# Softmax exponents moved ahead of a copy, a ranking round split by rows, and token factors in one piece, in the first stage of a fused attention kernel

## What is computed

```
Q = x @ Wq;  K = ctx @ Wk;  V = ctx @ Wv
scores = Q K^T / sqrt(32)                  # per head, 256 x 256
topv, topi = top_k(scores, 32)             # per row
probs = softmax(topv), scattered to topi   # the other 224 places are 0
c_t = mean over heads of probs, times V, times the text mask
x1 = layernorm(x) * (1 + gate*scale_in(c_t)) + gate*shift_in(c_t)
y  = s4d(x1)                               # a convolution over the whole sequence, by a DFT
xt = x + y * (1 + gate*scale_out(c_t)) + gate*shift_out(c_t)
out = layernorm(xt + gelu(layernorm(xt) @ W1 + b1) @ W2 + b2)
```

## Time and profile before

| | |
|---|---|
| median of 3 runs | 1389.21 us |
| the profiled execution, its own time | 1390.56 us |
| its span, first to last instruction | 1388.9 us |
| granted TensorE clock, mean over the span | 0.925 |
| busy: PE / DVE / ACT / POOL | 85% / 63% / 44% / 33% |
| first stage | from 0 to about 456 us of the span |
| start of turns 0, 1, 2, 3 (PE L1235) | 118.4, 152.8, 192.8, 231.5 us |
| start of turns 4, 5, 6, 7 | 271.5, 311.4, 350.1, 389.0 us |

### The profile page before, as it was taken

How to read it: one execution, slowest core, us unless ns; L and a number is a source line. 1 busy time by engine, 2 the same in 40 slices (tenths; PEclk the granted TensorE clock), 3 DMA queues, 4 the chain that set the end, 5 groups by cost and what they waited for, 6 DMA issues and landing times. The chain is left out here.

```text
span 1388.9 us, 24448 instructions
## 1 busy us (share of the span) xinstructions
PE 1181.3 (85%) x7032; PEld 854.2 (62%) x7032; DVE 876.4 (63%) x2513; ACT 611.6 (44%) x1242; POOL 451.4 (33%) x669
## 2 busy tenths in 40 slices
PE   1588799999896588789998949689999899999997
PEld 1385567777675477577766837456666555555554
DVE  7998888888842466656574647557676425353534
ACT  3545565666541223557763327256666521211120
POOL 2266144334446108837337337422220000000000
PEclk9858999999898899999999969779999999999999
DMA  9000000000000463486737516351010000000000
GB/s 280 9 2 1 1 1 1 1 1 1 1 1 1 111 221 100 136 269 217 261 112 254 171 45 106 92 146 16 9 17 1 1 1 1 15 0 15 0 16 16
DMA packets 92461, 91.98 MB, mean 66 GB/s; under 512 B 27056, under 2 KB 77746, under 8 KB 92340
## 3 DMA queue, kind: packets, MB, share of 16 engines
q1 hardware_dynamic: 80052, 65.32, 15.4%
q0 software_dynamic: 12288, 25.18, 7.1%
HBM read 75.79 MB, written 14.68 MB: 65 GB/s over the span
## 5 line engine op out<-in xcount | busy, mean ns | idle before, releaser
L3544 ACT ACTIVATE m_silu<-m_psG 128x512 f32<-128x512 f32 x48 | 28.7, 597 | 215.2 <-PE m_psU L3664 215.2
L3597 DVE TENSOR_TENSOR m_act<-m_silu,m_psU 128x512 f32<-128x512 f32 x48 | 33.0, 688 | 122.5 <-ACT m_silu L3544 107.7
L2304 PE MATMUL gq_psH<-gq_xT,gq_w 128*128 (+1 forms) x564 | 98.6, 300 | 5.2 <-issue 3.0
L2304 PEld LDWEIGHTS gq_psH<-gq_xT,gq_w 128*128 128x128 f32 x564 | 78.9, 200 | 31.0 <-issue 26.0
L2314 PE MATMUL gq_psY<-leaf_w,gq_hT 128*128 (+1 forms) x282 | 89.5, 400 | 7.2 <-DVE gq_hT L2190 6.8
L3664 PE MATMUL m_psG<-m_xnT,m_gate 128*128 128x512 f32 x192 | 92.0, 602 | 2.1 <-PEq L192 2.1
L3664 PE MATMUL m_psU<-m_xnT,m_up 128*128 128x512 f32 x192 | 90.6, 594 | 0.0
L2190 DVE SCALAR_TENSOR_TENSOR gq_hT<-gq_xT,unit_leaf,gq_act 128x128 f32<-128x128 f32 x141 | 49.6, 352 | 49.6 <-ACT gq_act L2022 33.0
L3075 DVE TENSOR_REDUCE c_max<-c_psA 128x4 f32<-128x1024 f32 x32 | 39.2, 1226 | 60.9 <-PE c_psA L3226 60.9
L1906 POOL DMA_INDIRECT gq_x<-rows_x,gq_token_i x48 | 46.2, 963 | 93.9 <-DVE gq_tile_row L2183 54.3
L205 POOL TENSOR_SCALAR m_rstd<-m_mean_var 128x4 f32<-128x4 f32 x4 | 0.9, 231 | 232.5 <-DVE m_mean_var L1389 232.5
(11 more groups left out here) (584 smaller groups left out, 3034.3 us busy)
## 6 DMA issues: line engine op xcount, KB each, us to landing
leaf_w<-in_group_w SPq DMA_DIRECT2D x128, 128.0 KB, 3.9
leaf_w<-in_group_w SPq DMA_DIRECT2D x64, 256.0 KB, 5.0
a_w<-in_L_xattn_W SPq DMA_DIRECT2D x2, 1024.0 KB, 11.9
rows_x<-token_rows SPq DMA_DIRECT2D x8, 256.0 KB, 5.2
sorted_y_q<-gq_y SPq DMA_DIRECT2D x16, 128.0 KB, 4.5
sorted_y_k<-rows_ahead SPq DMA_DIRECT2D x16, 128.0 KB, 5.4
sorted_y_v<-gq_y SPq DMA_DIRECT2D x16, 128.0 KB, 1.8
rows_f<-token_rows SPq DMA_DIRECT2D x8, 256.0 KB, 2.8
```

Source lines behind the costliest of these rows:

```text
L2304: last = pe.matmul(psH[n % 2][:, 0:P], w1[n % 3][:, c, :], xT[:, c, bass.ds(g * -P + u * P, P)], start=(c == 0), stop=(c == DC - 1))
```

## The change

On ScalarE `projected` is parted into `x_turned` (L656) and `projected` (L660), and the exponentials of the ranked scores now stand between the two, in two halves, each waiting for its own half of `ranked`. In round 3 on VectorE `ranked` is raised behind the fourth and the eighth MAX8; the shares are computed by halves: four takes, shares of half 0, two takes, shares of half 1, two takes. `scaled_shares` waits for each half of the shares by itself. On GpSimd the token factors of batches 0 to 6 are computed in one piece of 14 columns in turn 9; the piece at the end of turn 7 is gone. No other operation, shape or buffer changes, and no DMA. The convolution itself is not touched.

```diff
@@ -358,8 +358,8 @@
         v_ps, v_sb = sig("a_v_ps"), sig("a_v_sb")
         score_ps, score_sb = sig("a_score_ps"), sig("a_score_sb")
         first8, left, taken = sig("a_max"), sig("a_left"), sig("a_taken")
-        exps, ranked, etop_sb = sig("a_exps"), sig("a_ranked"), sig("a_etop")
-        shares, scaled, mean_sb = sig("a_shares"), sig("a_scaled", 2), sig("a_mean")
+        exps, ranked, etop_sb = sig("a_exps"), sig("a_ranked", 2), sig("a_etop", 2)
+        shares, scaled, mean_sb = sig("a_shares", 2), sig("a_scaled", 2), sig("a_mean")
         at_ps, at_sb = sig("a_attnT_ps"), sig("a_attnT_sb")
         ct_ps, ct_sb = sig("a_ctT_ps"), sig("a_ctT_sb")
         fin_ps, fout_ps, fout_sb = sig("a_film_in_ps"), sig("a_film_out_ps", ST), sig("a_film_out", ST)
@@ -500,7 +500,7 @@
                             do.mark(biased)
                         else:
                             biased.then_inc(last_biased, 1)
-                            next_factors(NEXT - 2, NEXT)
+                            next_factors(0, NEXT)
                         released(pool, o_sb, z)
                         root(1, o_var, o_rs, z)
                         if z == B - 1:
@@ -527,8 +527,6 @@
                         do(pool.tensor_tensor(yspec[:, 1, :], prod[:, 2, :], prod[:, 3, :],
                                               ALU.add))
                         pool.tensor_copy(yspec[:, 0, 0:1], yspec[:, 0, 0:1]).then_inc(y_sb.s, 1)
-                    if m == B - 1:
-                        next_factors(0, NEXT - 2)
 
                 pool.memset(core.ident[:], 0.0).then_inc(core.setup, 1)
                 pool.memset(core.ones_bf[:], 1.0).then_inc(core.setup, 1)
@@ -651,25 +649,28 @@
                                               bias=nmax[:, j:j + 1], scale=scale)
                     last.then_inc(exps.s, 1)
 
-                def projected(f):
+                def x_turned(f):
                     reached(act, xT_ps, f)
                     act.activation(xnT[:], pA[:], ACT.Copy).then_inc(xT_sb.s, 1)
+
+                def projected(f):
                     reached(act, proj_ps, f)
                     released(act, score_ps, f)
                     own = slice(0, 2 if f < 2 else 1)
                     act.activation(qk[:, own], pB[:, own], ACT.Copy).then_inc(proj_sb.s, 1)
 
                 def top_exponents(b):
-                    reached(act, ranked, b)
-                    for j in range(R):
-                        last = act.activation(etop[:, j, :], top[:, j, :], ACT.Exp,
-                                              bias=nmax[:, j:j + 1], scale=scale)
-                    last.then_inc(etop_sb.s, 1)
+                    for n in range(2):
+                        reached(act, ranked, b, n + 1)
+                        for j in range(n * HALF, (n + 1) * HALF):
+                            last = act.activation(etop[:, j, :], top[:, j, :], ACT.Exp,
+                                                  bias=nmax[:, j:j + 1], scale=scale)
+                        last.then_inc(etop_sb.s, 1)
 
                 def scaled_shares(b):
-                    reached(act, shares, b)
                     reached(act, exps, b)
                     for n in range(2):
+                        reached(act, shares, b, n + 1)
                         for j in range(n * HALF, (n + 1) * HALF):
                             last = act.activation(prob[:, j, :], prob[:, j, :], ACT.Copy,
                                                   scale=einv[:, j:j + 1])
@@ -738,9 +739,12 @@
                     if has(e):
                         gelus(e, range(HC // 2, HC))
                     if has(f):
+                        x_turned(f)
+                    if has(b):
+                        top_exponents(b)
+                    if has(f):
                         projected(f)
                     if has(b):
-                        top_exponents(b)
                         scaled_shares(b)
                     if has(f):
                         scores_out(f)
@@ -761,6 +765,7 @@
                 act.activation(tmask[:], tmask8[:], ACT.Copy, scale=1.0 / H0).then_inc(masks, 1)
                 x_normal(0)
                 values_out(0)
+                x_turned(0)
                 projected(0)
                 act.wait_ge(core.loads[0], 16)
                 sums(1)
@@ -769,6 +774,7 @@
                 film_folded()
                 x_normal(1)
                 values_out(1)
+                x_turned(1)
                 projected(1)
                 for n in range(B // 2 - 1):
                     keys_out(n)
@@ -819,7 +825,7 @@
                         do.wait_apart()
                     for j in range(R):
                         last = dve.max(top[:, j, 8 * r:8 * r + 8], row_in(r, j))
-                        if r == 3 and j == R - 1:
+                        if r == 3 and j % HALF == HALF - 1:
                             last.then_inc(ranked.s, 1)
                         else:
                             do.mark(last)
@@ -839,13 +845,14 @@
                     if signal is not None:
                         last.then_inc(signal.s, 1)
 
-                def shares_of(b):
-
-                    reached(dve, etop_sb, b)
-                    do(dve.tensor_reduce(einv[:], etop[:], AX_X, ALU.add))
-                    do(dve.reciprocal(einv[:], einv[:]))
-                    tm = tmask[:, b * ST:(b + 1) * ST].unsqueeze(1).to_broadcast([P, H0, ST])
-                    e3 = einv[:].rearrange("p (h t) -> p h t", h=H0)
+                def shares_of(b, n):
+
+                    q = slice(n * HALF, (n + 1) * HALF)
+                    reached(dve, etop_sb, b, n + 1)
+                    do(dve.tensor_reduce(einv[:, q], etop[:, q], AX_X, ALU.add))
+                    do(dve.reciprocal(einv[:, q], einv[:, q]))
+                    tm = tmask[:, b * ST:(b + 1) * ST].unsqueeze(1).to_broadcast([P, H0 // 2, ST])
+                    e3 = einv[:, q].rearrange("p (h t) -> p h t", t=ST)
                     dve.tensor_tensor(e3, e3, tm, ALU.mult).then_inc(shares.s, 1)
 
                 def pairs_of(b):
@@ -913,8 +920,10 @@
                         eight(b, 3)
                         reached(dve, ranked, b)
                         take(3, range(HALF))
-                        shares_of(b)
-                        take(3, range(HALF, R), taken)
+                        shares_of(b, 0)
+                        take(3, range(HALF, R - 2))
+                        shares_of(b, 1)
+                        take(3, range(R - 2, R), taken)
                         pairs_of(b)
 
                 def next_stats(first, end):
```

## The result

The changed kernel took **1367.01 us** (median of 4 runs, 1364.70 to 1368.11) beside 1388.57 us before (4 runs, 1385.67 to 1391.27): ratio 0.9843, interval 0.9819 to 0.9867, so 21.6 us less. In a later comparison (experiment 9) it took 1365.36 beside 1387.30, ratio 0.9838 [0.9816, 0.9861]. The forecast was 1373.5 in 1368 to 1382: the direction is right, the saving was forecast at 15.7 us and came out at 21.6, and the time lies 1.0 us under the range.

The account below looks back on a forecast made before the run. Neither PE nor DVE is full; they wait in turn, as exponentials stand behind L660. Terms 10.3+2.5+2.85-0.65+0.85-0.2-0.1+0.8 = 16.35 us off 1390.56 give 1374.2; forecast 1373.5, range 1368 to 1382.

Parts of the forecast that it names:

- Part 1: Turns 1 to 5: exponentials ahead of L660 let L1235 start right behind L1318, 2.06 us at five turn starts, 10.3 us.
- Even: Turn 6, likewise turn 0 (-0.1 us): DVE's second half set of shares costs about what the three short waits it replaces did.
- Part 2: Turns 2 to 5: with no gap PE's clock does not fall, 2.5 us gained, bounds 0 and 2.5.
- part 4: Entry and turn 0: L688 and the pipeline start earlier, 0.85 us; late scores in turn 0 -0.2, second half set -0.1.
- Part 3: Turn 6: at full clock DVE's wait for PE's L1137 goes, 2.85 us; a possible clock fall ahead of turn 7, -0.65.
- Part 5: Turn 8: without factors ahead of it on POOL the root of batch 7 starts earlier, 0.8 us; the 14-column piece costs nothing.
- The sum: All parts together: 16.35 us off the profiled execution of 1390.56, giving 1374.2.
- all in favour: Range's low end: every bound favourable saves 17.5 us, off the fastest run 1368.2.
- The clock falls anyway: Rival, chance 0.16: the gap may not cause the clock's falls, so parts 2 and 3 give nothing; 1377.6 to 1379.
- DVE becomes the bound: Rival, chance 0.08: L860's chain is slower than computed, the gap shrinks to about 1 us; 1383, about no change.
- The cut is not what ends the wait: Rival, chance 0.03: the scores' copy L682, not L860, ends L1235's wait; gap stays 1 or more, 1383 to 1388.
- The wait for ranks holds L660: Rival, chance 0.03: on ACT in turns 0 to 5 late ranks delay L660, scores and L1318; slower, 1400.

Follow-up runs that it names:

- experiment 9: The changed kernel itself, measured once more beside the kernel before: 1365.36 us, ratio 0.9838.
- experiment 1: The kernel before with only the copy of x and the exponentials moved ahead of L660, in one piece, factors as before: 1374.13 us, ratio 0.9906.
- 6: The changed kernel with L867, the sum of the shares, done once more for batches 2 to 6: 1367.68 us, ratio 0.9848.
- experiment 7: The changed kernel with L867, the sum of the shares, done 2.5 times more for batches 2 to 6: 1377.12 us, ratio 0.9912.
- 10: The changed kernel without halves: exponentials, shares and scaling in one piece each: 1372.93 us, ratio 0.9897.
- 2: The kernel before with ranks, exponentials and shares in halves, L660 still ahead of the exponentials, factors as before: 1374.12 us, ratio 0.9899.
- 8: The changed kernel with L660 ahead of the exponentials again in turn 0 alone: 1369.97 us, ratio 0.9868.
- 11: The changed kernel with L660 ahead of the exponentials in turn 0 alone, same code as 8, measured again: 1368.61 us, ratio 0.9865.
- experiment 3: The kernel before with only the token factors changed, one piece of 14 columns at the last root: 1386.70 us, ratio 0.9987.
- 4: The kernel before plus nine idle matmuls of PE behind L1318 in turns 0 to 6: 1391.39 us, ratio 1.0031.
- experiment 5: The kernel before plus four idle matmuls of PE behind L1318 in turns 0 to 6: 1381.96 us, ratio 0.9956.

## Why the prediction was right, and where it missed

**What bounds the kernel: right.** The exponentials stood behind L660 and nothing else kept them; experiment 1 shows it by the order alone, and 6 and 7 that DVE is then about 1 us ahead.

**Part 1 (10.3 us): right in kind, 1.2 us small.** The gap of 2.06 is gone at all five starts. A turn was to be 36.63 and is 36.39: back to back, L1244 overlaps L1327 by 0.14 to 0.16 and is 0.07 shorter, 5x0.24 = 1.2 us. The half set of shares was put at 0.75 and takes 0.60 from start to the next instruction (217.71 to 218.31); the cover was right all the same. The Trainium skill, page "VectorE: DVE Perf Modes", section on the TRN2 errata, states a fixed cost of about 150 cycles per instruction, from which the prediction worked out an estimate of 0.61; the trace's 0.60 for the three together agrees. "Even" was wrong for what a second half set costs in turns 0 and 6: there the halves give 1.8 and 0.7 us (experiments 9, 10). In turns 1 to 5 they give nothing, so that the part of the change with the most lines serves two turns of seven.

**Part 2 (2.5 us): right in kind, one turn short.** The clock no longer falls from the end of turn 0 to turn 8. But I counted turns 2 to 5. Turn 1 had a fall too. PE of the kernel before at the start of turn 1:

```profile
152.84 3.25 PE L1235 MATMUL a_psW<-identity,s_Z_re_a_pair 128*128 128x128 f32 x16 [4.21 <-DVE s_Z_re_a_pair L860]
```

The same 16 matmuls take 2.02 at full clock; the row was there to be read, and is 1.2 us of turn 1's surplus. What ended it was part 4's own step: the late scores, which I charged with -0.2, push L1327 back until L1244 follows it at once. PE is about as idle in turn 0 as before, but ahead of the scores, which wait for L660 (8.32 us, in place of 4.41 ahead of L1318 and 4.21 behind it). The gap of 4.2 us need not bring a fall each time: behind 3.57 and 3.51 there was none (experiments 2 and 8), behind 3.85 there was (11).

**Part 3: 2.85 was 3.41; -0.65 was 0.** Turn 6 ran at full clock all through, and DVE waits nowhere for the film-in product (L908) there, as forecast. But it is the end of one fall that is won here: the kernel before lost it in one of two profiles (38.87 against 35.72 in experiment 3), so 3.41 is what is gained where the fall had come, and 0.26 where it had not. The gap ahead of turn 7 came (1.62, forecast "some 2"), but no fall behind it. That gap is shorter than 2.06, and experiments 2 and 7 had none behind 1.10 to 1.65 either.

**Part 4: 0.85 was about 0.4, turn 0 as forecast.** L1191 does start 0.87 earlier than in experiment 3, which has the old entry (109.77 against 110.64). Yet turn 0 begins at 117.83 and 117.84. Two windows between these times show why; the granted clock is the third figure from the end. The changed kernel:

```profile
115.49:116.47 0.98, 0.98 (x3) 0.70 (x3) 0.98 (x3) 0.00 (x0) 0.84 (x2) 0.50 0.00 0
```

Experiment 3:

```profile
115.49:116.47 0.98, 0.98 (x5) 0.80 (x5) 0.95 (x2) 0.62 (x1) 0.84 (x2) 1.00 0.00 0
```

PE works here at half clock in one and at full clock in the other: what came earlier ran at half clock, and for 0.98 us longer. Where the rise comes at nearly the same time (114.43 in experiment 9, 114.25 in 10), 0.82 us earlier at L1191 leaves 0.35 at turn 0. Over all profiles turn 0 begins on average at 117.54 in the seven profiles with the halves and at 117.94 in the six without, within a scatter of 2 us. So the term is about 0.4: the early start counts half, since it lies at half clock.

**Part 5 (0.8 us): right in kind.** The root starts as forecast. The 0.78 in the two profiles has the size of their scatter: turns 7 to 9 take 66.8 to 67.9 us in the eight profiles with the one piece and 67.7 to 69.1 in the five without.

**The sum.** Against 16.35: 1.2 for the shorter turns, 1.2 for turn 1's clock, 0.55 in turn 6, 0.65 not lost ahead of turn 7, 0.2 in turn 0, less 0.3 at the entry, give 19.85 of stage one's 19.93. The 3.4 us of later stages are the profiles' scatter. The step that failed is **the range's low end, and in it the upper bounds of parts 1 and 2**: "all in favour" took 17.5 us off the fastest run of before. Part 1 had no room upward, and each turn gave 0.24 more; part 2 was held to turns 2 to 5 and put turn 1's clock at nothing without a reason, though its slow L1235 stands in the trace, and it gave 1.2. With these the saving would have been bounded by 19.9 and the low end would have been 1365.8, under the 1367.0 measured. That is the profiles' account. The medians have 21.6 and 21.9 us; what the other runs gained beyond stage one's 16.8 to 19.9 stays open.

**The rivals.** "The clock falls anyway" is refuted by 4 and 5. "DVE becomes the bound" has its point of decision a little further off than it was put, 1.0 to 1.3 us away in place of 0.8 to 1.1; the changed kernel stays on the near side but for turns 6 and 0. "The cut is not what ends the wait" is refuted by 1, where only the order was changed and the gap closed. "The wait for ranks holds L660" did not happen in turns 1 to 5: L660 waited 0.4 us in all; in turn 0 it was late as forecast (144.38, forecast 144.5), without harm.

## What to carry to other kernels

When an instruction that is ready stands behind one that waits, on an engine that is mostly idle, move it ahead: one exchange of two calls alone gave 13.6 of the 21.6 us. A gap of 2 us per turn on TensorE costs more than its length, since the clock can fall behind it and slow the first matmuls of the next turn; so count a gap together with the slow first group behind it, in every turn, and don't trust one profile for it: two profiles of the same code had their falls in other turns, 3.15 us apart in turn 6. Before two edits that serve the same wait are added up, ask which of them is left with work once the other is in: here 13.6 and 13.6, with about 1 for the factors, made 21.6.

## What the runs showed of the hardware that was not expected

- **The clock falls behind some gaps and not behind like ones, and shorter gaps were safe.** By the length of PE's gap ahead of a turn: 2.06 us, a fall in 5 of 10 cases (kernel before and experiment 3, starts of turns 2 to 6); 1.10 to 1.82, in none of 18 (1.61 to 1.65 nine times, experiment 7 and ahead of turn 7 of the changed kernel, 6, 8, 9 and 11); 2.33 to 2.36, in one of 3 (5; not in 1 and 10); 3.51 and 3.57, in neither (8 and 2); 3.85 to 4.21, in all 3 (11, 3 and the kernel before). So length alone does not decide. The Trainium skill, page "TensorE: Matmul & The Clock Gate", Part 1, says of the rise to full clock that the same kernel makes it after different numbers of matmuls from run to run. It says so of the start of a kernel; here the fall varies in the same way: 8 and 11 are the same code, with turns of 36.47 and 37.70 us.
- **Idle matmuls paid.** Four of them per turn, 1.7 us of work that nobody uses, gained 5.2 us in experiment 5 (0.9956 [0.9938, 0.9974]), since they lay in a gap; nine, 3.9 us, cost 0.31%.
- **An earlier start can be given back to the clock.** PE's work came 0.87 us earlier at the entry and ended at the same time, as full clock came at 116.47 in one profile and at 115.49 in the other; with the rise 0.18 apart (9 and 10), 0.82 us earlier left 0.35.
- **Small powers on GpSimd cost by the column:** L206 takes 0.72 us for 2 columns and 2.61 for 14, in the changed kernel: about 0.16 a column and 0.4 fixed.
